# Shared inner weights of a mixture-of-experts stage in room of their own, split inside the tile loop; one product dealt out among the last tiles; the first pair of a projection reordered

## The reference

```python
# layer 0, attention: 32 heads, 8 KV heads, HEAD_DIM 128
kv = concatenate([context, latents], axis=1)
q, k = rms_norm(latents @ Wq), rms_norm(kv @ Wk);  v = kv @ Wv
out = softmax(q @ k.T * scale) @ v @ Wo          # per group of 4 heads
# layer 0, ffn: gate, up, down with ternary weights, rounded to int8
inter = silu(gate) * up;  inter_q = trunc(clip(inter * 128, -128, 127))
# layer 1, attention over the context, without weights
sim = softmax(key @ query * KC ** -0.5);  context = sim @ value
# layer 1, ffn: 16 routed experts, 2 per token, and a shared one of 2 x 128
scores = softmax(x @ router_w + router_b) + router_bias   # top 2 groups, top 2 experts
shared = (silu(x @ sw1 + sb1) * (x @ sw2 + sb2)) @ sw3 + sb3
```

## Time and profile before

| | |
|---|---|
| time, median of 3 runs | 1226.1 us (1225.43 to 1226.37) |
| the profiled execution, its time | 1224.71 us |
| its span, first to last instruction | 1223.0 us |
| mean granted TensorE clock | 0.986 |
| busy: PE, PEld | 1169.9 us (96%), 1005.2 us (82%) |
| busy: DVE, ACT, POOL | 832.4 us (68%), 588.2 us (48%), 348.8 us (29%) |
| chain that ended last | PE 59%, DVE 21%, issue 9%, ACT 5%, POOL 2%, DMA 2% |

### The profile page before, as it was taken

One profiled execution on the slowest core, in us unless ns is written; L12 is line 12 of the kernel. 1 busy time (PEld: TensorE's weight loads), 2 busy tenths in 40 slices (PEclk: granted clock), 3 DMA queues, 4 the chain that ended last, 5 costly groups with the idle time before them and its releaser, 6 DMA issues.

```text
span 1223.0 us, 20618 instructions
## 1 busy us (share of the span) xinstructions
PE 1169.9 (96%) x6956; PEld 1005.2 (82%) x6956; DVE 832.4 (68%) x2373; ACT 588.2 (48%) x1364; POOL 348.8 (29%) x302
## 2 busy tenths in 40 slices
PE   7899999999999999999999999998999999899992
PEld 6798888988889888889888888887887777578871
DVE  6767667666676666676676776669788878784334
ACT  4545455454545545555454545445444455524441
POOL 5313022221312312132130321203343312445661
PEclk8999999999999999999999999999999999999996
DMA  7011000000101100010010000001212323833435
GB/s 275 1 36 52 2 35 18 35 34 0 51 0 34 31 20 34 0 51 0 34 51 0 34 0 1 1 1 54 83 55 74 106 69 103 321 126 126 144 103 206
DMA packets 37465, 73.57 MB, mean 60 GB/s; under 512 B 6098, under 2 KB 22482, under 8 KB 35366
## 3 DMA queue, kind: packets, MB, share of 16 engines
q1 hardware_dynamic: 30726, 56.38, 13.3%
q0 software_dynamic: 4960, 12.33, 3.2%
q10 hardware_dynamic: 1728, 4.20, 0.9%
HBM read 64.50 MB, written 12.32 MB: 63 GB/s over the span
## 4 chain that ended last, share of the span: by engine, by line
PE 59%; DVE 21%; issue 9%; ACT 5%; POOL 2%; DMA 2%; SPq 1%; DVEq 0%; ACTq 0%; POOLq 0%
PE bank L354 14%; PE bank L356 14%; PE bank L355 14%; PE bank L1978 5%; PE bank L1847 3%; DVE probs L1159 3%; ACT probs L790 3%; PE bank L1688 2%; PE bank L1989 2%; DVE k_junk L1116 2%; DVE iq L1322 2%; DVE row_max L1132 2%; DVE pt_lo L1146 2%; POOL k_rstd L577 1%; PE bank L1630 1%
## 5 line engine op out<-in xcount | busy, mean ns | idle before, releaser
L790 ACT ACTIVATE probs<-bank,exp_bias,q_rstd 128x256 f32<-128x256 f32 x256 | 141.3, 562 | 138.0 <-DVE exp_bias L1140 138.0
L1151 DVE TENSOR_TENSOR o_lo<-bank,o_hi 128x512 fp32r<-128x512 f32 x64 | 44.3, 692 | 178.6 <-ACT o_hi L783 178.6
L354 PE MATMUL bank<-wkv_hi,kv_src_lo 128*128 128x256 f32 x512 | 145.8, 285 | 1.4 <-DVE kv_src_lo L1184 1.4
L355 PE MATMUL bank<-wkv_lo,kv_src_hi 128*128 128x256 f32 x512 | 145.6, 284 | 0.0
L356 PE MATMUL bank<-wkv_hi,kv_src_hi 128*128 128x256 f32 x512 | 145.5, 284 | 0.0
L581 POOL TENSOR_TENSOR q_rstd<-q_var,minus_half 128x8 f32<-128x8 f32 x32 | 52.7, 1646 | 300.4 <-DVE q_var L1119 300.4
L779 ACT ACTIVATE pt_hi<-bank 128x512 fp32r<-128x512 f32 x128 | 69.6, 596 | 116.2 <-PE bank L1688 116.2
L354 PE MATMUL bank<-wo_hi,o_lo 128*128 128x512 f32 x256 | 104.2, 407 | 1.7 <-DVE o_lo L1151 1.2
L577 POOL TENSOR_TENSOR k_rstd<-k_var,minus_half 128x4 f32<-128x4 f32 x32 | 32.5, 1016 | 249.1 <-DVE k_var L1093 249.1
L354 PE MATMUL bank<-wq_hi,kv_src_lo 128*128 128x512 f32 x256 | 102.8, 401 | 0.8 <-POOL wq_lo L566 0.8
L356 PE MATMUL bank<-wo_hi,o_hi 128*128 128x512 f32 x256 | 101.5, 397 | 0.0
(11 more groups left out here) (257 smaller groups left out, 3090.6 us busy)
## 6 DMA issues: line engine op xcount, KB each, us to landing
weights<-r_w SPq DMA_DIRECT2D x16, 768.0 KB, 9.3
wq_raw<-wq SPq DMA_DIRECT2D x8, 1024.0 KB, 4.7
wo_raw<-wo SPq DMA_DIRECT2D x8, 1024.0 KB, 4.8
wkv_raw<-wkv SPq DMA_DIRECT2D x8, 512.0 KB, 3.3
gu_raw<-w_gate SPq DMA_DIRECT2D x10, 256.0 KB, 3.4
gu_raw<-w_up SPq DMA_DIRECT2D x10, 256.0 KB, 3.8
wd_raw<-w_down SPq DMA_DIRECT2D x10, 256.0 KB, 4.1
x_sb<-x SPq DMA_DIRECT2D x4, 512.0 KB, 9.8
```

The lines of the kernel that those rows point to most:

```text
L354: eng.matmul(out_ap, a_lo, b_hi, start=start, stop=False)
L355: eng.matmul(out_ap, a_hi, b_lo, start=False, stop=False)
L790: act.activation(probs[:, h, :], scores_ps[h // 2][:, (h % 2) * 256:(h % 2) * 256 + 256], ACT.Exp, bias=exp_bias[:, h:h + 1], scale=q_rstd ...
L1151: dve.tensor_tensor(o_lo[:, par, :], o_ps[:, :], o_hi[:, par, :].bitcast(F32), ALU.subtract)\
```

## The change

Seven edits.

1. `e12_hi` and `e12_lo` move out of the room of `iq` to that behind `s_raw`, where the ffn's split gate and up weights were, free once TensorE has finished with them (`gu_done`).
2. `expert_high` becomes `inner_high` (in s = 2 and s = 4 of the tile loop) and `outer_high` (in s = 9, behind `down_done`). GpSimd's `inner_low` goes to s = 3 and s = 5, behind `first_rows` of the same step.
3. The first product, `inner_part(0, 0)`, writes bank 5 (`inner_bank`) and is dealt out: chunks 0 and 1 in s = 7, chunk 2 ahead of the similarity of s = 8 and chunk 3 behind it. Before, all four stood behind `context` of s = 8. `route(1)`, also in bank 5, waits for `silu_ready`, and `silu_of(0)` moves to s = 8.
4. Blocks 4 to 6 of the routed weights overlap the new room. They are loaded last, behind blocks 0 and 1, when `h_done` says that the shared inner products are over.
5. VectorE adds `add_shared(4)` and `(5)` ahead of `take_weights(0)` and `(1)`, and does `gate_slots` in the middle of the routed tiles.
6. At the start VectorE does the first half of `q_norm`, `rows_pair(3)`, `k_low`, `q_low`, and only then the second half. `low_pair(3)` goes behind the first `bias_of`.
7. TensorE no longer waits for six low parts (`ln_lo_ready[0]`, 6) in the first group.

```diff
+        at[0] = gu_at + SHARED * EW * 4
         e12_hi = put("e12_hi", [P, 2, 2 * KC, P], F32R)
         e12_lo = put("e12_lo", [P, 2, 2 * KC, P], F32R)
+        at[0] = inner_at + 2 * SHARED * 2 * D * 4
...
+        def inner_bank(n, i):
+
+            return bank[5] if n == 0 and i == 0 else bank[2 * shared_order[n][0] + i]
...
-            sp.wait_ge(gu_done, 4 * CH)
-            load_weights(4, 6)
...
-            load_weights(6, 14)
+            load_weights(7, 14)
...
             load_weights(0, 2)
+            load_weights(4, 7)
...
-                else:
-                    inner_low(s - NB)
+                if s in (3, 5):
+                    pool.wait_ge(ln_row_ready[0], 2 * NB + s + 1)
+                    inner_low((s - 3) // 2)
...
-            def expert_high(e):
+            def inner_high(e):
                 act.wait_ge(s_loaded, 16 * SHARED)
+                act.wait_ge(gu_done, 4 * CH)
...
-                if s == NB - 1:
+                if s in (2, 4):
+                    inner_high((s - 2) // 2)
+                if s == NB:
+                    silu_of(0)
+                if s == NB + 1:
                     act.wait_ge(down_done, NB)
-                    expert_high(0)
-                if s == NB:
-                    expert_high(1)
-            silu_of(0)
+                    for e in range(SHARED):
+                        outer_high(e)
...
-            q_norm(0)
+            q_norm(0, range(0, 1))
             rows_pair(3)
             k_low(0, 0)
             q_low(0, 0, 0)
+            q_norm(0, range(1, 2))
+            q_low(0, 1, 0)
             low_pair(2)
-            q_low(0, 1, 0)
-            low_pair(3)
...
                     bias_of(n, b)
+                    if isinstance(g, int) and g == 0 and b == 0:
+                        low_pair(3)
...
+            add_shared(4)
+            add_shared(5)
             take_weights(0)
             take_weights(1)
-            add_shared(4)
-            add_shared(5)
-            gate_slots()
...
-                        if isinstance(g, int) and g == 0 and b == 0:
-                            pe.wait_ge(ln_lo_ready[0], 6)
...
-                pe.wait_ge(down_cut, 4 * (NB - 2 + half) + 2)
+                if half == 0:
+                    pe.wait_ge(down_cut, 4 * (NB - 2) + 2)
+                else:
+                    pe.wait_ge(silu_ready, 1)
...
                 if 0 <= s - 1 < NB:
+                    if s == NB:
+                        inner_part(0, 0, range(2, 3))
                     similarity(s - 1)
                 if 2 <= s + 1 < NB:
                     down(s + 1, 8, CH)
+                if s == NB - 1:
+                    pe.wait_ge(down_cut, 4 * (NB - 1) + 2)
+                    inner_part(0, 0, range(0, 2))
+                if s == NB:
+                    inner_part(0, 0, range(3, KC))
...
-                if s == NB:
-                    pe.wait_ge(ln_hi_ready[0], 3 * NB - 1)
-                    inner_part(0, 0)
```

More of the change, by code:

```diff
@@ L656, in inner_low @@
             def inner_low(e):
-                pool.wait_ge(e_hi_ready, e * 2 + 2)
+                pool.wait_ge(e_hi_ready, e + 1)
                 pool.tensor_tensor(e12_lo[:, e, :, :].rearrange("p c n -> p (c n)"), s_raw[:, e, 0:2 * D],
@@ L662, in outer_low @@
             def outer_low(e):
+                pool.wait_ge(e_hi_ready, SHARED + e + 1)
                 pool.tensor_tensor(e3_lo[:, e, :], s_raw[:, e, 2 * D:EW], e3_hi[:, e, :].bitcast(F32),
@@ L914, in _, with outer_high @@
             chunks(act, inner_chunk)
-            def expert_high(e):
+            def inner_high(e):
                 act.wait_ge(s_loaded, 16 * SHARED)
+                act.wait_ge(gu_done, 4 * CH)
                 act.activation(e12_hi[:, e, :, :].rearrange("p c n -> p (c n)"), s_raw[:, e, 0:2 * D], ACT.Copy)\
                    .then_inc(e_hi_ready, 1)
+            def outer_high(e):
                 act.activation(e3_hi[:, e, :], s_raw[:, e, 2 * D:EW], ACT.Copy).then_inc(e_hi_ready, 1)
@@ L927, in silu_of @@
                     act.wait_ge(h_lo_ready, n - 1)
-                act.activation(e_h[:, n % 2, :], bank[2 * e][:, :], ACT.Silu, bias=b12[:, e, 0:1]).then_inc(silu_ready, 1)
+                act.activation(e_h[:, n % 2, :], inner_bank(n, 0)[:, :], ACT.Silu, bias=b12[:, e, 0:1]).then_inc(silu_ready, 1)
             def hidden_high(n):
@@ L1105, in k_low, with q_norm @@
                    .then_inc(k_lo_ready, 1)
-            def q_norm(pair):
-                for i in range(2):
+            def q_norm(pair, tiles=range(2)):
+                for i in tiles:
                     dve.wait_ge(q_copied, pair * 2 + (i + 1))
@@ L1117, in q_norm @@
                                                  q_ss[:, i * R + h:i * R + h + 1]).then_inc(q_ss_ready, 1)
+                if tiles[-1] == 0:
+                    return
                 dve.wait_ge(q_ss_ready, pair * 8 + 8)
@@ L1520, in hidden @@
                 dve.wait_ge(h_done, 2 * n + 2)
-                dve.scalar_tensor_tensor(out=e_h[:, n % 2, :], in0=bank[2 * e + 1][:, :], scalar=b12[:, e, 1:2],
+                dve.scalar_tensor_tensor(out=e_h[:, n % 2, :], in0=inner_bank(n, 1)[:, :], scalar=b12[:, e, 1:2],
                                          in1=e_h[:, n % 2, :], op0=ALU.add, op1=ALU.mult).then_inc(h_ready, 1)
@@ L1584, in _ @@
                     take_weights(j + 2)
+                if j == TILES // 2:
+                    gate_slots()
             for t in range(NB):
@@ L1897, in inner_part @@
                 for k in chunks:
-                    mm = three(pe, bank[2 * e + i][:, :], e12_hi[:, e, i * KC + k, :], e12_lo[:, e, i * KC + k, :],
+                    mm = three(pe, inner_bank(n, i)[:, :], e12_hi[:, e, i * KC + k, :], e12_lo[:, e, i * KC + k, :],
                                xt_hi[:, k, tok], xt_lo[:, k, tok], k == 0, k == KC - 1)
```

## The result

The changed kernel takes 1222.24 us (median of nine; eight lie between 1219.77 and 1222.81, and one took 4581 us at a mean granted clock of 0.245; without it the median is 1221.82), the kernel before 1226.58 in the same series: a ratio of 0.9958 without that execution, 95% interval 0.9945 to 0.9971, so 0.42% faster. The profiled execution is the median one; its span is 1220.5 us. Against the 1224.71 us of the profile before it gained 2.5, where 6.4 were forecast. To see where, I followed the same instructions through both traces and noted how much earlier each starts: 3.2 us at the second pair of the first group, 3.2 still before the last tiles, 7.3 at the first `x_cols`, 4.3 at the second tile's, 2.4 at the last `y_rows`. So there are two gains and two losses.

What follows compares the result with a forecast made beforehand. The prediction took TensorE to be busy nearly throughout, so edits pay only where it stands or the chain runs through another engine. Start 2.1 plus last tiles 4.3 gave 6.4 us off: 1219.7 us, range 1218.0 to 1223.0.

Steps and rivals of the forecast that it cites:

- The start: First pair: reordering brings `k_lo` forward and `exp_bias` ends at 36.7 instead of 38.84, gaining 2.1 us, bounds 0 and 3.2.
- the row at 60.83: Earlier `exp_bias`, 1.31 us, ending with the third of GpSimd's four operations; taken to show VectorE getting in between two.
- 10.3 us after it resumed: Start: TensorE's products for pair 1 keep their old pace after the `k_lo` stop, so from 30.5 they end at 40.8.
- The last tiles: End of tile loop: no `e_lo` beside `moe_rows`, tile 7's done at 1054.65 instead of 1058.99, gaining 4.3 us; bounds 2.3, 4.8.
- Splitting inside the loop: Tile loop: ScalarE's copies in s = 2 and 4 and GpSimd's `e_lo` cost nothing, else up to 0.5 us each.
- The weights: Before the routed tiles: five blocks land at 1089.3, wanted at 1092.2, costing nothing; the rival that they are late had 0.07.
- `gate_slots`: Moved from before the routed tiles to among them: nothing gained, nothing lost.
- The copies are caught: Rival before the routed tiles: GpSimd's four additions keep the `block_w` copy out, 1.8 us lost, 1221.5 us; chance 0.20.
- The clock: Rival: TensorE's 2.0 us stop before tile 7's transposes lowers the granted clock, costing 1.6 us, 1221.3 us; chance 0.08.

Runs made afterwards that it cites:

- section 2: Kernel before with only the reordered first pair: 1220.57 us, ratio 0.9963; changed kernel with the old order of the first pair: 1223.06 us, ratio 0.9986.
- section 5: Changed kernel with the first shared product in one piece: 1220.03 us, ratio 0.9969; with one `e_lo` back beside `moe_rows` of tile 6: 1221.99 us, ratio 0.9983.
- section 3: Changed kernel with `take_weights(0)` and `(1)` back ahead of VectorE's `add_shared(4)` and `(5)`: 1226.82 us, ratio 1.0007 to the kernel before.
- the changed kernel's two traces: Changed kernel unaltered, traced in the first series (1222.24 us, kernel before 1226.58) and again as yardstick (1219.71 us, kernel before 1224.76, ratio 0.9962).

## Why the prediction was right, and where it was off

The sign and the range hold (1222.24 in 1218.0 to 1223.0; forecast 1219.7). That it is so near is in part luck: the start gave 0.85 more than forecast and the copies, which the sum left out, took 1.5 to 3.05. By its steps:

- **The start, 2.1 us**: 2.95 measured. The order worked as forecast, and `exp_bias` used the gap between the two `ctx_low`, as the row at 60.83 had suggested. It ended at 35.92 instead of 36.7: I had `q_var` at 32.2 and `q_rstd` at 1.88 us, they came at 31.63 and 1.65. But the 2.1 was taken from the wrong path. What sets the second pair is TensorE's products, as section 2 shows, and the mis-sized step is "10.3 us after it resumed". That pace held the low clock behind the old stop. By it the products would have ended at 40.8, 1.6 earlier than the 42.38 before, and the second pair could not have gained 2.1. They took 9.0 us, since the clock stayed up behind the shorter stop. Of the 2.95, 1.56 is the earlier `k_lo` (1.83 less 0.27 from the loading of x) and 1.4 the faster products. The granted clock was 1.00 from 30 to 38 us in all twelve traces with the new order and fell in both with the old one. The prediction looked for the clock at the other end only.
- **The last tiles, 4.3 us**: 4.1 measured, the 0.2 being the new wait of `moe_rows` for a store. The share is shown by the two kernels of section 5: most of it is the two `moe_rows` that GpSimd no longer stops, and 0.4 the dealing.
- **Splitting inside the loop, nothing**: right. The shift before and behind the two places differs by under 0.1 us; `down_whole` came up to 0.4 late and caught up.
- **The weights**: forecast to land at 1089.3 and wanted at 1092.2, they landed by 1087.8 and were wanted at 1088.6, so 0.8 us were to spare instead of 2.9. That the old order of the copies would have been late is shown by section 3.
- **`gate_slots`, nothing**: shown, for the kernel in which GpSimd waits for the copies.
- **The failed step is the order of the likelihoods.** "The copies are caught" had 0.20 and happened in each of the six traces in which the additions weren't held back. I weighed two rows, `gates` (kept out through four additions) and `exp_bias` at 60.83 (let in), as if they were two outcomes of one case. They weren't: the `gates` row had the same neighbour as the copy would have, GpSimd's `add_shared`, and the other had a different one. And I placed the request "within a few tenths" of the additions without asking which came first; both follow the same chain, so it was the same 0.2 us in each of the five traces with this order (0.16 to 0.20). Price: 1.8 forecast, 1.5 measured without the clock, 2.9 to 3.05 with it.
- **The clock**, a rival with 0.08 for the stop ahead of tile 7: it stayed up there (2.16 and 2.25 us of standing) in the changed kernel's two traces and fell in two others with 1.96 and 2.35. It fell ahead of the first routed product instead, in four of the five traces with the caught copy, one of the changed kernel's two among them.

The sum, put right, for the first trace: 3.2 + 4.1 - 3.05 - 1.9 = 2.4 of the 2.5 measured. For the second: 3.5 + 4.1 - 1.5 + 0.9 = 7.0 (the routed stage 92.81 instead of 93.67), and 1224.71 - 1217.84 = 6.9.

## What to carry to other kernels

When an operation of VectorE is moved, look at what GpSimd does in that half microsecond; a row in which the *same* neighbour keeps VectorE out is worth more than any number of rows with another one, and an order that is decided by 0.2 us on one chain is no coin toss. When a pace is read from a row, read the granted clock beside it: a stop that the change shortens can give back the clock as well, 1.4 us here. Where a row of GpSimd operations isn't urgent, one wait that puts it behind the urgent copy costs nothing and makes the time independent of who comes first. And one profile of each kernel was not enough to size a change of 0.5%: the clock behind one stop and a few stray stops moved single executions by 3 us.

## What the hardware showed that I had not expected

- A copy that is waiting doesn't get its turn from GpSimd's additions: asked for 0.2 us behind the first (1089.55) or 0.2 ahead of it during a gather's issue (1088.38), it waited for all four, 5.3 to 5.7 us in six traces. With 0.14 us between the additions it got in after the first. But `ctx_low` twice in a row, as closely packed, let `exp_bias` in, and two of these additions let `r_mult` in between them (1.41 us). Which operations are let in I haven't settled; all that were let in were another operation or had another neighbour. The Trainium skill (SBUF — State Buffer, "SBUF: two separate sides") says that whoever starts first gets the ports for the whole instruction. The trace agrees for a single instruction (2.39 us beside one `e_lo`), but for a row of them the rule doesn't tell who is next.
- The granted clock fell to 1.2 GHz behind stops of TensorE of 1.8 us in four traces, one of them of the changed kernel, and stayed at 2.4 GHz behind 1.8 us in the other trace of the same code; behind stops of 2.0 to 2.5 us at tile 7 it went either way too (it fell in two traces, with 1.96 and 2.35, and stayed up in seven). Where it fell behind the 1.8, it cost some 1.4 to 1.5 us.
- The gathers and the weights share the transfer engines, and the last packets of the weights trailed the bulk by 1.5 to 2 us: 89% of the engines' time until 1085.0, then two to seven packets each half microsecond until 1087.0, in the trace of section 3.
